# Dense graph attention: every second step's fourth head is built by VectorE and GpSimd together

## The reference, cut to what matters

```python
e = leaky_relu(el[src] + er[dst], 0.2)      # one score per edge and head
ex = exp(e - segment_max(e, dst)[dst])
a = ex / segment_sum(ex, dst)[dst]
out = segment_sum(a[:, :, None] * feat[src], dst)
```

## Time and profile before

| | us |
|---|---|
| median of 3 runs | 3004.75 |
| lowest, highest | 3004.15, 3007.91 |
| the profiled execution | 3003.86 |
| its span, first to last instruction | 3002.2 |
| VectorE busy in L1099, 1200 instructions | 796.7 |
| TensorE busy in L1167, 7200 instructions | 789.8 |

### The profile page before, as it was taken

The page is one execution under the profiler, slowest core; times in us unless marked ns, Lnnn a source line. Parts: engine busy times, 40 slices in busy tenths (PEclk is TensorE's granted clock), DMA queues, the critical chain, the costliest instruction groups (busy, mean ns, idle before and its releaser), DMA issues. The chain is left out here.

```text
span 3002.2 us, 50772 instructions
## 1 busy us (share of the span) xinstructions
PE 2495.9 (83%) x17111; PEld 1245.4 (41%) x17164; DVE 2350.3 (78%) x5375; ACT 1158.3 (39%) x2327; POOL 1364.5 (45%) x1627
## 2 busy tenths in 40 slices
PE   5999979999969999966997947677676777767598
PEld 3666655333355333344665512233332333323365
DVE  6888889999959999977444847777777777777477
ACT  5777720000020000012222435666666666566421
POOL 2999920000000000001830867777777777775055
PEclk8999989999989999976998977888888888888799
DMA  4000000000020000031432687888888888888343
GB/s 125 12 11 12 10 36 15 15 15 15 5 82 15 15 15 15 5 100 45 121 96 64 203 249 238 250 259 256 259 255 252 257 257 260 255 252 250 121 150 107
DMA packets 210756, 373.53 MB, mean 124 GB/s; under 512 B 52554, under 2 KB 140559, under 8 KB 208682
## 3 DMA queue, kind: packets, MB, share of 16 engines
q0 software_dynamic: 75536, 238.14, 26.4%
q1 hardware_dynamic: 131737, 128.66, 13.5%
q10 hardware_dynamic: 3200, 3.21, 0.4%
HBM read 324.84 MB, written 50.04 MB: 125 GB/s over the span
## 5 line engine op out<-in xcount | busy, mean ns | idle before, releaser
L1167 PE MATMUL dense_p_o<-dense_W,feat 128*32 128x512 f32 x7200 | 789.8, 595 | 17.5 <-DVE dense_W L1099 17.5
L1099 DVE SCALAR_TENSOR_TENSOR dense_W<-layer_B,steep,cnt 128x512 f32<-128x512 f32 x1200 | 796.7, 750 | 3.3 <-DVE dense_W L1099 2.0
L2466 POOL DMA_INDIRECT Wd<-tab_d,ixq x544 | 519.4, 955 | 171.1 <-issue 166.2
L1167 PEld LDWEIGHTS dense_p_o<-dense_W,feat 128*32 128x32 f32 x7200 | 281.9, 110 | 494.5 <-issue 390.3
L1577 POOL MEMSET edst<- 128x782 int32 x1 | 0.8, 750 | 921.9 <-POOLq L1216 921.9
L2644 PE MATMUL strips_p_sg<-strips_sv,strips_oh 128*32 128x512 f32 x2000 | 313.6, 704 | 101.0 <-DVE strips_sv L2509 101.0
L2632 PE MATMUL strips_p_b<-strips_wrs,strips_ohT 96*128 96x256 bf16 x1000 | 177.8, 308 | 208.8 <-DVE strips_ohT L2480 190.6
L732 POOL TENSOR_SCALAR mix_L<-mix_back,encode_lowT 128x128 bf16<-128x128 f32 x520 | 328.6, 650 | 18.7 <-PE mix_p_c L891 18.6
L2573 ACT ACTIVATE strips_p_s<-strips_tv 128x1024 f32<-128x1024 f32 (+1 forms) x250 | 225.2, 901 | 157.3 <-DVE strips_sv L2509 144.5
L1123 ACT COPY dense_part<-dense_p_o 128x512 f32<-128x512 f32 x36 | 18.8, 596 | 639.7 <-PE dense_p_o L1167 639.7
L2466 POOL DMA_INDIRECT strips_G<-tab_d,ixq x240 | 228.9, 954 | 73.1 <-issue 72.8
(11 more groups left out here) (543 smaller groups left out, 3899.3 us busy)
## 6 DMA issues: line engine op xcount, KB each, us to landing
strips_row<-dlr_d SPq DMA_DIRECT2D x250, 96.0 KB
ew<-in_ew SPq DMA_DIRECT2D x16, 1024.0 KB, 5.4
layer_B<-rise_d SPq DMA_DIRECT2D x12, 1024.0 KB, 4.6
hx_d<-hrow SPq DMA_DIRECT2D x24, 512.0 KB, 2.7
Wd<-tab_d,ixq POOLq DMA_INDIRECT x544
Wd<-in_fWd SPq DMA_DIRECT2D x8, 1024.0 KB, 9.2
tab_d<-feat SPq DMA_DIRECT2D x50, 130.0 KB, 1.9
tab_d<-gated_in_rowg SPq DMA_DIRECT2D x25, 256.0 KB, 2.0
```

Source lines behind the costliest of these rows:

```text
L1099: o = nc.vector.scalar_tensor_tensor(out=out, in0=rise, scalar=C.steep[:, q * H + h:q * H + h + 1], in1=count, op0=ALU.max, op1=ALU.mult)
L1167: m = nc.tensor.matmul(p_o[c % 2][h * MT:(h + 1) * MT, a, 0:n], feat[:, q, h, lo:lo + MT], W[t % 3][:, h, 0:n], start=(q == 0), stop=(q == ...
L2466: gp.indirect_dma_start(out=G[n % RING][:, j, :], out_offset=None, in_=C.tab3[:, :], in_offset=bass.IndirectOffsetOnAxis(ap=index, axis=0) ...
```

## The change

In the steps with odd q (12 of 25) the fourth head's tile is made in two parts. VectorE writes the maximum alone, with a `tensor_scalar` (counted by `s_top`); GpSimd multiplies the tile in place by the counts (`s_Wp`). The counts that GpSimd reads are a bf16 copy `whole` of the bytes, which ScalarE makes for each of these steps (`s_whole`), in a single buffer, so that a copy waits for the product before it. ScalarE's copies stand between its `take` and `keep`: those for q = 1 ahead of `take`, for q = 3 behind it, for q = 5 between the second and third `keep`, the rest behind the fourth. TensorE waits for `s_Wp` instead of `s_W` at the fourth head of these steps. `ready(t, h)` works out the numbers to wait for.

```diff
+        whole = sb("whole", [P, DC], BF16)
+        def helped(q):
+            return q % 2 == 1
...
@@ vector, for q, for h
-                                o = nc.vector.scalar_tensor_tensor(out=out, in0=rise, scalar=C.steep[:, q * H + h:q * H + h + 1], in1=count,
-                                                                   op0=ALU.max, op1=ALU.mult)
-                                o.then_inc(s_W, 1)
+                                if helped(q) and h == H - 1:
+                                    nc.vector.tensor_scalar(out, rise, source, None, ALU.max).then_inc(s_top, 1)
+                                else:
+                                    nc.vector.scalar_tensor_tensor(out=out, in0=rise, scalar=source, in1=count, op0=ALU.max, op1=ALU.mult).then_inc(s_W, 1)
...
+            @block.gpsimd
+            def _(gp):
+                with when_near(C, gp, 1):
+                    for t in range(full * NB):
+                        if helped(t % NB):
+                            n = ready(t, H - 1)[1]
+                            gp.wait_ge(s_top, n)
+                            gp.wait_ge(s_whole, n)
+                            nc.gpsimd.tensor_tensor(W[t % 3][:, H - 1, :], W[t % 3][:, H - 1, :], whole[:, :], ALU.mult).then_inc(s_Wp, 1)
...
+                    def counts(c, qs):
+                        for q in qs:
+                            k = ready(c * NB + q, 0)[1]
+                            if k >= 2:
+                                act.wait_ge(s_Wp, k - 1)
+                            nc.scalar.copy(whole[:, :], C.cnt[:, q, c * DC:c * DC + DC]).then_inc(s_whole, 1)
...
                     for c in range(full):
+                        further = c + 1 < full
+                        if further:
+                            counts(c + 1, [1])
                         take(c)
-                        keep(c)
+                        if further:
+                            counts(c + 1, [3])
+                        keep(c, 0, 2)
...
+                                        if helped(q) and h == H - 1:
+                                            pe.wait_ge(s_Wp, by_gp)
+                                        else:
+                                            pe.wait_ge(s_W, by_v)
```

More of the change, by code:

```diff
@@ L1057, in stage_attend_dense, with ready @@
         feat = C.feat[:, :].rearrange("p (b h d) -> p b h d", h=H, d=HW)
+        s_Wp = sem("s_Wp"); s_top = sem("s_top"); s_whole = sem("s_whole")
+        whole = sb("whole", [P, DC], BF16)
+        def helped(q):
+            return q % 2 == 1
+        def ready(t, h):
+            c, q = divmod(t, NB)
+            help_before = c * len([1 for k in range(NB) if helped(k)]) + len([1 for k in range(q) if helped(k)])
+            return t * H - help_before + h + 1, help_before + 1
         full, last = N // DC, N % DC
@@ L1098, in _ @@
                                 count = C.cnt[:, q, c * DC:c * DC + n].rearrange("p (b d) -> p b d", d=P)
-                                o = nc.vector.scalar_tensor_tensor(out=out, in0=rise, scalar=C.steep[:, q * H + h:q * H + h + 1], in1=count,
-                                                                   op0=ALU.max, op1=ALU.mult)
-                                o.then_inc(s_W, 1)
-                        v.wait_ge(s_W, (c + 1) * NB * H)
+                                source = C.steep[:, q * H + h:q * H + h + 1]
+                                if helped(q) and h == H - 1:
+                                    nc.vector.tensor_scalar(out, rise, source, None, ALU.max).then_inc(s_top, 1)
+                                else:
+                                    nc.vector.scalar_tensor_tensor(out=out, in0=rise, scalar=source, in1=count, op0=ALU.max, op1=ALU.mult).then_inc(s_W, 1)
+                        v.wait_ge(s_W, ready((c + 1) * NB, 0)[0] - 1)
+                        v.wait_ge(s_top, ready((c + 1) * NB, 0)[1] - 1)
                         v.sem_inc(s_used, 1)
@@ L1123, in take, with keep @@
                             nc.scalar.copy(part[:, a, 0:n], p_o[c % 2][:, a, 0:n]).then_inc(s_part, 1)
-                    def keep(c):
-                        for b in range(blocks(c)):
+                    def keep(c, first, end):
+                        for b in range(first, min(end, blocks(c))):
                             u = c * (DC // P) + b
@@ L1133, in keep @@
                                 nc.scalar.copy(to[:, :, lo:hi], p_r[u % 2][0:rows, a, :].rearrange("p (h d) -> p h d", h=H)[:, :, MT - (hi - lo):MT]).then_inc(s_acc, 1)
+                    def counts(c, qs):
[4 more added lines that the diff above has]
+                            nc.scalar.copy(whole[:, :], C.cnt[:, q, c * DC:c * DC + DC]).then_inc(s_whole, 1)
+                    counts(0, [q for q in range(NB) if helped(q)])
                     for c in range(full):
+                        further = c + 1 < full
+                        if further:
+                            counts(c + 1, [1])
                         take(c)
-                        keep(c)
+                        if further:
+                            counts(c + 1, [3])
+                        keep(c, 0, 2)
+                        if further:
+                            counts(c + 1, [5])
+                        keep(c, 2, 4)
+                        if further:
+                            counts(c + 1, [q for q in range(6, NB) if helped(q)])
                     act.wait_ge(s_pad, 1)
```

2 lines of the change are left out of this document (1 added, 1 removed).

## The result

The changed kernel takes 3264.52 us (median of 4; 3255.02 to 3267.21), where the kernel before takes 3005.18. The ratio is 1.0856, 95% interval 1.0832 to 1.0879. The forecast was 3081, the range 3040 to 3165: the direction was right, the loss is 259 us and not 77.

A forecast was written before the change was run, and what follows sets the result against it. VectorE (66.4 us a chunk) and TensorE (66.7) were taken as nearly level bounds. VectorE's chunk would become 58.4 + 3.5 + 11.2 = 73.1 us, adding 77 us over both layers to 3003.86: 3081 us, range 3040 to 3165.

The forecast's parts named there:

- The ceiling: Dense stage: TensorE needs 66.7 us of a chunk's 66.84, which limits any gain from a lighter VectorE.
- VectorE's maximum: Helped fourth-head tile: VectorE's `tensor_scalar` takes 0.37 us, 0.29 after overlap, instead of 0.664; bounds 0.145 and 0.664.
- GpSimd's product: Helped tile: GpSimd's 512-column multiplication by the counts takes 1.18 us; bounds 0.667 and 1.69.
- VectorE's loss on one: Each of 12 products in a chunk takes 0.93 us out of VectorE's time by mutual exclusion, 1.18 less 0.25.
- the forecast's sum: VectorE's chunk: 58.4 for 88 tiles, 3.5 for 12 maxima, 11.2 for 12 products, 73.1 us instead of 66.4.
- take turns: GpSimd's product gets in between two VectorE instructions without a wait between them, VectorE losing 0.6 to 1.2 us; chance 0.7.
- only when VectorE stands: Rival: GpSimd's product stands until VectorE waits for a buffer; 190 us more, 3195 us; chance 0.09.
- The rival's own working: With products served only when VectorE waits for a buffer, six steps take 19.8 us, 3.31 a step instead of 2.67.
- The casts at nothing: ScalarE's 144 casts of counts cost nothing; at most 0.3 us late once a chunk, for q = 7.
- The clock: TensorE's granted clock stays at 1.00 in the dense stage; a fall to 0.84, giving 3157 us, had chance 0.1.
- theory D: From the follow-up runs: a product loses its turn when VectorE's next instruction was handed to the engine before GpSimd asks.

The follow-up runs named there:

- relief: Changed kernel without GpSimd's product and ScalarE's casts, VectorE still writing the maximum alone and TensorE waiting for it: 3004.2 us, 0.9983 of the kernel before.
- write: Changed kernel with two GpSimd memsets of the same tile, which only write SBUF, in place of each product: 3005.1 us, 0.9991 of the kernel before.
- psum: Changed kernel with VectorE's tiles taking their second input from PSUM ones instead of SBUF counts, and one PSUM transpose buffer instead of two: 3010.3 us, ratio 1.0000.
- turn: Changed kernel with VectorE waiting, in the step behind a helped one, ahead of its second tile until its first is complete: 3099.8 us, ratio 1.0306.
- cast4: Changed kernel with four buffers for the copied counts and the casts for q = 1, 3, 5, 7 of the next chunk ahead of `take`: 3214.5 us, ratio 1.0689.
- turn_cast4: Changed kernel with both VectorE's gap ahead of the second tile and the four count buffers with early casts: 3098.5 us, ratio 1.0294.
- short_lead: Changed kernel with a VectorE wait ahead of the second tile behind a helped step, but on the maximum two instructions back: 3180.1 us, ratio 1.0575.
- void_wait: Changed kernel with a VectorE wait ahead of the second tile behind a helped step, on a TensorE count already waited for, so never holding: 3190.2 us, ratio 1.0609.
- late_gap: Changed kernel with a gap on VectorE ahead of the fourth tile, not the second, of the step behind a helped one: 3117.5 us, ratio 1.0365.
- fourth_turn: Changed kernel with only every fourth step helped, six products in a chunk, and VectorE's gap behind each: 3051.2 us, ratio 1.0147.

## Why the prediction was wrong

- **The ceiling: right.** "Even if VectorE's work were free, TensorE would hold the pitch at 66.7 of 66.84": relief has 66.84.
- **VectorE's maximum: 0.29 us forecast, 0.39 measured.** 144 x 0.1 = 14 us of the sum were missing; the two rows it was drawn from the earlier trace rows have other shapes of the input; whether that is the reason no run shows.
- **GpSimd's product: 1.18 forecast, 1.16 measured. VectorE's loss on one: 0.93 forecast, 0.91 measured.** The rows of mutual exclusion gave the right size, and write and psum show its terms. With the measured sizes the forecast's sum is 58.4 + 4.7 + 10.9 = 74.0 us a chunk; turn has 74.38 and 3099.8 us. As a price of the exclusion the sum was right to 19 us.
- **That VectorE and GpSimd take turns: this step failed.** The forecast drew it from one case, L2010, L1893 and L2011, and gave "only when VectorE stands" 0.09. Of the 65 products that asked just behind the start of a tile, 40 stood, 35 of them for 5.96 us. Removing the standing gives 116 us between cast4 and turn_cast4, and 165 from the changed kernel to turn. The rival's own working, three products in six steps of which the first stands, the second goes at once and the third gets in at a short wait, is what the trace shows where it happens: 5.96, 1.16, 1.72 us. Its pitch, 82.8 us, is near cast4's (83.2, from 504.48 to 920.35 in five chunks), but that is luck: the working has every third product stand, four in a chunk, at full clock, and cast4 has 25 in 12 chunks, with a clock that fell. I had the mechanism and its price and gave it far too little weight.
- **The casts at nothing: failed behind the first.** Their cover was worked out for a TensorE that is not late. Behind a product that stood it is late by some 5 us, the turns with it, and the casts with these. It costs 50 us on top of the standing and, as turn against turn_cast4 shows, nothing without.
- **The clock:** the forecast had 1.00 in the stage. In the stretches from 500 to 820 us it was 0.89 to 0.94 in the changed kernel and 0.91 to 0.97 in cast4, where TensorE stands for 3.0 to 5.4 us behind a standing product, and 1.00 in turn, where TensorE is busy 93% of the time. So the fall is a consequence of the standing, but it adds a cost of its own.

No run removes that cost by itself, but two products of the changed kernel, at 788.06 and 877.50, allow a comparison. Both are the second of their chunk, both stand for 5.96 us, and TensorE stands for 2.98 and 3.01 us. VectorE's next tile, TensorE's matmuls up to its next turn, and the stretches in them (the granted clock is the third number from the end), first for the one and then for the other:

```profile
799.44 0.75 DVE L1114 SCALAR_TENSOR_TENSOR dense_W<-layer_B,steep,cnt 128x512 f32<-128x512 f32 x1 [6.43 <-PE dense_p_o L1213]
...
886.31 2.08 DVE L1114 SCALAR_TENSOR_TENSOR dense_W<-layer_B,steep,cnt 128x512 f32<-128x512 f32 x3 [3.86 <-PE dense_p_o L1213]
```

```profile
794.08 5.33 PE L1213 MATMUL dense_p_o<-dense_W,feat 128*32 128x512 f32 x18 [2.98 <-POOL dense_W L1136]
...
883.51 2.76 PE L1213 MATMUL dense_p_o<-dense_W,feat 128*32 128x512 f32 x18 [3.01 <-POOL dense_W L1136]
```

```profile
793.00:799.00 6.00, 4.92 (x18) 0.95 (x18) 0.01 (x1) 0.00 (x0) 1.02 (x1) 0.50 0.00 0
883.00:886.00 3.00, 2.49 (x18) 0.64 (x18) 0.00 (x0) 0.00 (x0) 0.46 (x1) 1.00 0.00 0
```

At 0.50, the 1.2 GHz level, the same 18 matmul records take 5.33 us instead of 2.76, and VectorE waits 6.43 us instead of 3.86. Behind the 35 long products VectorE waits 198 us in all; at 3.86 each it would be 135. So an estimate of what the fallen clock adds is 63 us in the changed kernel, and in the same way 44 us in cast4 (141 us of waits behind 25 products). The working of the rival had no such term: its VectorE waited only as long as TensorE needs at full clock.

The parts, in the order of the runs: relief to turn_cast4, the mutual exclusion with the gap, 94 us; turn_cast4 to cast4, standing, 116 us with the clock in it; cast4 to the changed kernel, late casts and ten more products that stand, 50 us, again with the clock in it.

**What stays open.** What decides whether a product gets in between two tiles that follow without a gap. It is not the time of asking: standing and served products ask alike, 0.15 to 0.17 us after the start of a tile. It is not settled by VectorE's sequencer being held (short_lead) nor by one more instruction in its stream (void_wait), though both make it rarer. But the place in the chunk matters: among the products that asked in this way with no gap right behind the tile, the first of a chunk (q = 1) always stood, 7 of 7 in the changed kernel, 11 of 11 in cast4 and in void_wait, 12 of 12 in late_gap and in short_lead. Of the other 132 products of short_lead only 3 stood, of late_gap's none. So theory D falls for the first products and is not refuted for the rest, and no run here tests what sets the first ones apart.

No version here beats the kernel before with the whole computation in it. The best that keeps the product in every second step is the one with the gap and four buffers, 1.0294; relief shows that the most to be had from a lighter VectorE is 0.2%.

## What to carry to other kernels

Before work moves from one engine to another, work out the pace of the engine behind it: here TensorE held a chunk at 66.84 us where VectorE needed 66.4, and no relief could have paid. A read of GpSimd beside VectorE instructions with two SBUF inputs was no parallel work here (0.91 us lost for a product of 1.16), and next to a VectorE without gaps 35 of 144 products were not served until VectorE ran out of buffers. If the two must share, give VectorE a gap where GpSimd asks, and price the case of no turns as high as the case of turns unless a row shows many in a row. And price what the engine behind does after it has stood: here its clock fell to 0.50, and that was an estimated 63 of the 259 us.

## What the runs showed of the hardware

- A product of GpSimd with two SBUF inputs costs VectorE's two-input instructions 0.91 us of its 1.16. The Trainium skill ("SBUF — State Buffer", section "Who interferes with whom") says that a VectorE instruction with two SBUF inputs contends with a GpSimd instruction that reads SBUF and not with one that only writes it, and that one with a single SBUF input, outside the two-port modes, does not contend. The runs agree on both sides: two memsets of 0.53 us inside tiles that take 4.73 us for seven, and a product of 1.16 us inside seven tiles of 4.70 us with one input in PSUM.
- Not expected: the one that comes second is not sure to be next. 35 of 144 products stood through eight instructions of VectorE, 4.8 us, and so did 25 in cast4. A gap on VectorE right behind the tile, which costs 0.12 us where a product has already got in (5.75 us for seven tiles in late_gap, 5.63 without it), ended it wherever it was tried: 72 of 72 products end within 1.61 us in fourth_turn, and so do the 65 listed in turn.
- After TensorE had stood for 3.0 to 5.4 us behind a product of 5.96 us, its granted clock was 0.50 for a while in 30 of 35 cases, and 18 matmul records then took 5.33 us instead of 2.76.
- A `tensor_scalar` of 128x512 f32 takes 0.476 us, less than a `scalar_tensor_tensor` of the same shape (0.750) and more than half of it.
